# Gathers shared out between two stages, and a dense stage of a graph network rebuilt around centred matmul outputs

## The reference

```python
h = relu(layernorm(x)); x = x + L0(h, node_type, src, dst, etype, ...)  # typed attention, softmax over a node's edges
h = relu(layernorm(x)); x = x + L1(h, proj_cosim, W_ffn, b_ffn, src, dst)  # relu(h_diff @ W_ffn.T + b_ffn)
h = relu(layernorm(x)); x = x + L2(h, edge_index, W0, b0, W1, b1)
h = relu(layernorm(x)); x = x + L3(h, Wq, ..., Wf, bf, gamma, beta, src, dst)

def L2(x, edge_index, W0, b0, W1, b1):
    h = x + segment_sum(x[src], dst)
    return relu(h @ W0 + b0) @ W1 + b1

def L3(feats, ...):                       # o: attention over the edges, 0 for a node without any, + bo
    h = feats @ Wf + bf + o
    return h + (h - mean(h)) * rsqrt(var(h) + 1e-5) * gamma + beta
```

## Time and profile before

| | us |
|---|---|
| median of 3 runs | 6195.22 (6193.31 to 6201.44) |
| the profiled execution | 6195.52, span 6193.7 |
| tables | 0 to 167 |
| dense | 167 to 1397 |
| scores | 1400 to about 2407 |
| granted clock, mean | 0.788 of 2.4 GHz |

### The profile page before, as it was taken

One profiled execution on the slowest core, in us unless ns is written; L12 is line 12 of the kernel. 1 busy time (PEld: TensorE's weight loads), 2 busy tenths in 40 slices (PEclk: granted clock), 3 DMA queues, 4 the chain that ended last, 5 costly groups with the idle time before them and its releaser, 6 DMA issues. The chain is left out here.

```text
span 6193.7 us, 73617 instructions
## 1 busy us (share of the span) xinstructions
PE 5013.1 (81%) x19049; PEld 2686.4 (43%) x19049; DVE 4517.1 (73%) x7949; ACT 2488.5 (40%) x7048; POOL 3864.5 (62%) x3983
## 2 busy tenths in 40 slices
PE   0899489988999996999978886666688877878886
PEld 0455245544555553566644443222233334444443
DVE  4788377767888886999966665666688766666666
ACT  0788367763333332455533332222233333333333
POOL 1777787764444441000058887888788857777787
PEclk9999688889999998999965555555688866777666
DMA  9333145543333332999943333444566622222221
GB/s 357 109 105 105 34 134 136 136 119 80 81 80 79 81 80 46 277 286 285 285 108 83 83 83 79 115 114 114 121 164 165 156 75 66 65 65 64 63 59 41
DMA packets 868574, 739.52 MB, mean 119 GB/s; under 512 B 568092, under 2 KB 575218, under 8 KB 868032
## 3 DMA queue, kind: packets, MB, share of 16 engines
q1 hardware_dynamic: 566112, 525.53, 29.8%
q0 software_dynamic: 102464, 90.84, 8.1%
q10 hardware_dynamic: 199584, 118.45, 6.3%
HBM read 461.89 MB, written 276.55 MB: 119 GB/s over the span
## 5 line engine op out<-in xcount | busy, mean ns | idle before, releaser
L1298 POOL DMA_INDIRECT df_hs<-u,keep_idx x396 | 510.0, 1288 | 829.4 <-POOLq L209 709.1
L832 POOL DMA_INDIRECT sc_xg<-t,keep_gather x396 | 466.2, 1177 | 546.1 <-DVE sc_h L194 413.8
L748 POOL DMA_INDIRECT t<-keep_ptr_pay,keep_scat_ptr x396 | 472.1, 1192 | 253.4 <-issue 128.8
L1298 POOL DMA_INDIRECT hd_gat<-u,keep_idx x396 | 487.2, 1230 | 157.0 <-issue 115.2
L758 POOL DMA_INDIRECT den_xd<-t,keep_gather x396 | 474.3, 1198 | 122.3 <-issue 115.8
L1831 POOL DMA_INDIRECT out_x<-hd_x,keep_scat_out x396 | 451.0, 1139 | 146.7 <-issue 119.1
L1298 POOL DMA_INDIRECT pr_gat<-sd,keep_idxsd x396 | 411.8, 1040 | 88.8 <-issue 70.8
L1298 POOL DMA_INDIRECT ml_gat<-u,keep_idx x396 | 401.1, 1013 | 98.6 <-issue 70.3
L629 ACT ACTIVATE den_dh<-den_den_dn_cent,den_den_dn_rstd 128x64 f32<-128x64 f32 x1584 | 397.8, 335 | 4.8 <-DVE den_den_dn_rstd L609 0.5
L1287 PE MATMUL at_ps_m<-at_vx,keep_msg_twice 128*128 128x512 f32 x792 | 364.2, 603 | 24.4 <-DVE at_vx L1178 24.4
L981 PE MATMUL sc_ps_r<-sc_qx,keep_weights 128*64 128x512 f32 x792 | 361.1, 598 | 1.0 <-DVE sc_prod L896 1.0
(11 more groups left out here) (297 smaller groups left out, 13083.3 us busy)
## 6 DMA issues: line engine op xcount, KB each, us to landing
u<-den_dh SPq DMA_DIRECT2D x198, 256.0 KB
t<-tab_row ACTq DMA_DIRECT2D x99, 272.0 KB, 11.3
tab_x<-in_x SPq DMA_DIRECT2D x99, 256.0 KB
den_dx<-in_x SPq DMA_DIRECT2D x99, 256.0 KB
out_x<-den_dx SPq DMA_DIRECT2D x99, 256.0 KB
sc_et<-in_etype_row SPq DMA_DIRECT2D x99, 256.0 KB
at_v<-vt SPq DMA_DIRECT2D x198, 128.0 KB, 5.4
at_et<-in_etype_row SPq DMA_DIRECT2D x99, 256.0 KB
```

Of the source, the lines that this page charges most:

```text
L748: pool.indirect_dma_start(pairs, bass.IndirectOffsetOnAxis(ap=e.scat_ptr[:, c:c + 1], axis=0), e.ptr_pay[:, c, :], None, bounds_check=NP * ...
L832: pool.indirect_dma_start(xg[i][:, u, :], None, e.T0, bass.IndirectOffsetOnAxis(ap=e.gather0[:, b.n, u:u + 1], axis=0), bounds_check=NP - ...
L1298: pool.indirect_dma_start(gat[i][:, u, :], None, table, bass.IndirectOffsetOnAxis(ap=idx_all[:, c:c + 1], axis=0), bounds_check=rows - 1, ...
```

## The change

**POOL and SP.** EARLY = 56 of the 99 groups of target gathers stay in dense, the other 43 (LATE, spread evenly, never two neighbours) go to scores, where POOL gathers them straight into the slot that DVE reads, behind the group's four source gathers; SP no longer loads such a group from XD but stores it there, since a later stage reads it. In dense the scatters and gathers run without waiting for the steps, with six buffers instead of three, and SP's stores of gathered rows begin at step 66 instead of 49.

The diff, cut to its core:

```diff
@@ constants and tables
+EARLY = 56
+LATE = [b for b in range(NG) if b * (NG - EARLY) // NG != (b + 1) * (NG - EARLY) // NG]
...
+                def exact_thirds(to, half, bias):
+                    link(v.tensor_copy(left[:, :], bias))
+                    link(v.memset(total[:, :], 0.0))
+                    for third in range(3):
+                        link(v.tensor_copy(piece[:, :], left[:, :]))
+                        link(v.tensor_copy(wide[:, :], piece[:, :]))
+                        link(v.tensor_tensor(left[:, :], left[:, :], wide[:, :], ALU.subtract))
+                        link(v.scalar_tensor_tensor(out=total[:, :], in0=wide[:, :], scalar=e.C["ident"][:, third:third + 1],
+                                                    in1=total[:, :], op0=ALU.mult, op1=ALU.add))
+                    link(v.tensor_copy(to[:, :, half, :], total[:, :].unsqueeze(1).broadcast_to([P, TU, D])))
...
@@ Dense.vector
         if part == 0:
+            if self.on(f1):
+                n3.recip(v, f1)
             if self.on(d):
...
+            if self.on(f1):
+                k = RN - self.ON_V
+                v.scalar_tensor_tensor(out=self.h3[f1.s][:, k:RN, :], in0=self.c3[f1.n % 2][:, k:RN, :], scalar=0.0,
+                                       in1=n3.rstd[:, k:RN].unsqueeze(2).broadcast_to([P, RN - k, D]),
+                                       op0=ALU.max, op1=ALU.mult).then_inc(self.h3_rows, 1)
...
+                v.tensor_tensor(self.c3[f.n % 2][:, :, :], self.ps_m[:, :, 1, :], self.c2[f.s][:, :, :], ALU.add).then_inc(self.c3_done, 1)
...
-                v.tensor_tensor(self.x2b[d.s][:, :, :], self.x2[:, :, :], self.rows(e.W["b1_row"]), ALU.add).then_inc(self.x2b_done, 1)
...
-                n3.total(v, self.x3[f.s][:, :, :]).then_inc(n3.chain, 1)
...
-                n3.shift(v, self.x3[f.s][:, :, :])
@@ Dense.tensor
                 for j in range(RN):
                     a, c = j % 2, j // 2
-                    m = pe.matmul(self.ps_m[:, j, :], self.hid[:, a, c * P:(c + 1) * P], e.W["w1"],
-                                  start=(j == 0), stop=(j == RN - 1), skip_group_check=True)
+                    if j % 4 == 0:
+                        pe.matmul(self.ps_m[:, j:j + 4, :, :], e.ones3[:, :], e.bias_m[:, :, :, :], start=True, stop=False,
+                                  skip_group_check=True)
+                    m = pe.matmul(self.ps_m[:, j, :, :], self.hid[:, a, c * P:(c + 1) * P], e.w1_pair[:, :, :],
+                                  start=False, stop=(j % 4 == 3), skip_group_check=True)
...
-                busy_with(pe, e, self.ps_idle, 3)
...
-                    pe.matmul(self.ps_h[:, 4 * bank:4 * bank + 4, :, :], e.C["ones"][0:1, :], self.e.bias_h[0:1, :, :, :],
+                    pe.matmul(self.ps_h[:, 4 * bank:4 * bank + 4, :, :], e.ones3[:, :], e.bias_h[:, :, :, :],
                               start=True, stop=False, skip_group_check=True)
@@ dense, SP
+        head = count * 66 // 99
+        def stored_at(n):
+            m, of = n - head, count - head
+            return range(len(early) * m // of, len(early) * (m + 1) // of) if 0 <= m < of else range(0)
@@ scores, POOL and SP
+                    if b.n in LATE:
+                        wait(pool, type_kept, b.n - (U - 1), e.pool_passed)
+                        wait(pool, xd_out[i], 16 * (late_of(b.n) - 1), e.pool_passed)
+                        for u in range(TU):
+                            pool.indirect_dma_start(xg[i][:, TU + u, :], None, e.T0,
+                                                    bass.IndirectOffsetOnAxis(ap=e.gather0[:, b.n, TU + u:TU + u + 1], axis=0),
+                                                    bounds_check=NP - 1, oob_is_err=False).then_inc(dst_in[i], 16)
...
+                    if b.on() and b.n in LATE:
+                        wait(sp, dst_in[b.s], 16 * TU * late_of(b.n), e.sp_passed)
+                        sp.dma_start(edge_rows(e.XD, b.n * GE, TW), xg[b.s][:, TU:R, :]).then_inc(xd_out[b.s], 16)
```

More of the change, by code:

```diff
@@ L195, in relu_to, with __init__, over, square @@
                                       op0=ALU.max, op1=ALU.mult)
+class Small:
+    def __init__(self, s, name, rows=RN):
+        self.rows = rows
+        self.sum, self.ss, self.std, self.rstd = [s.sb(f"{name}_{n}", [P, rows]) for n in ("sum", "ss", "std", "rstd")]
+        self.sq = s.sb(f"{name}_sq", [P, rows, D])
+        self.squared, self.summed, self.rooted, self.inverted = [
+            s.sem(f"{name}_{n}") for n in ("squared", "summed", "rooted", "inverted")]
+    def over(self, small):
+        return small[:, :].unsqueeze(2).broadcast_to([P, self.rows, D])
+    def square(self, a, cent, st):
+        wait(a, self.summed, st.n)
+        a.activation(self.sq[:, :, :], cent, ACT.Square).then_inc(self.squared, 1)
+    def sumsq(self, v, st):
+        v.wait_ge(self.squared, st.n + 1)
+        wait(v, self.rooted, st.n)
+        v.tensor_reduce(self.ss[:, :], self.sq[:, :, :], AX, ALU.add).then_inc(self.summed, 1)
+    def root(self, a, st, eps):
+        a.wait_ge(self.summed, st.n + 1)
+        wait(a, self.inverted, st.n)
+        a.activation(self.std[:, :], self.ss[:, :], ACT.Sqrt, bias=eps, scale=1.0 / D).then_inc(self.rooted, 1)
+    def recip(self, v, st):
+        v.wait_ge(self.rooted, st.n + 1)
+        v.reciprocal(self.rstd[:, :], self.std[:, :]).then_inc(self.inverted, 1)
 class Scope:
@@ L225, in norm @@
         return Norm(self.sb, self.sem, f"{self.tag}_{name}", rows)
-def busy_with(pe, e, ps, n):
-    for _ in range(n):
-        pe.matmul(ps[:, :], e.idle[:, 0:P], e.idle[:, :], start=True, stop=True)
 def edge_rows(table, at, width=D):
@@ L568, in vector @@
                 v.wait_ge(self.x2_done, d.n + 1)
-                n2.total(v, self.x2[:, :, :]).then_inc(n2.chain, 1)
+                wait(v, self.c2_done, d.n)
+                v.tensor_reduce(n2.sum[:, :], self.x2[d.s][:, :, :], AX, ALU.add).then_inc(self.total2, 1)
             if self.on(g):
@@ L575, in vector @@
             if self.on(g):
[L576 to L577 removed]
+                n4.recip(v, g)
             if self.on(d):
[L579 to L581 removed]
+                v.wait_ge(self.total2, d.n + 1)
+                wait(v, self.h2_done, d.n - (U - 1))
+                wait(v, self.c3_done, d.n - (U - 1))
+                v.scalar_tensor_tensor(out=self.c2[d.s][:, :, :], in0=n2.over(n2.sum), scalar=-1.0 / D,
+                                       in1=self.x2[d.s][:, :, :], op0=ALU.mult, op1=ALU.add).then_inc(self.c2_done, 1)
             if self.on(g):
[L583 removed]
+                v.wait_ge(n4.inverted, g.n + 1)
                 v.tensor_tensor(self.f1[:, :, :], self.ps_h[:, :, 0, :], n4.over(n4.rstd), ALU.mult).then_inc(self.f1_done, 1)
@@ L623, in scalar, with scale_rows @@
         eps = e.C["eps"]
-        def scale_rows(n, h, b, out, done):
-            a.wait_ge(n.chain, 2 * b.n + 2)
+        def scale_rows(n, cent, h, b, out, done, rows):
+            a.wait_ge(n.inverted, b.n + 1)
             wait(a, out[b.s], 16 * b.k)
-            for j in range(RN):
-                m = a.activation(h[b.s][:, j, :], n.cent[:, j, :], ACT.Relu, scale=n.rstd[:, j:j + 1])
+            for j in range(rows):
+                m = a.activation(h[b.s][:, j, :], cent[:, j, :], ACT.Relu, scale=n.rstd[:, j:j + 1])
             m.then_inc(done, 1)
@@ L863, in _ @@
                         wait(sp, sems[i], 16 * (NG // U), e.sp_passed)
+                for i in range(U):
+                    wait(sp, xd_out[i], 16 * late_of(NG - U + i), e.sp_passed)
             @block.vector
```

184 lines of the change are left out of this document (91 added, 93 removed).

## The result

| us | before | after |
|---|---|---|
| median on the same chip | 6194.5 (6193.3 to 6201.4) | 5954.2 (5951.3 to 5958.5) |
| the profiled execution | 6195.5 | 5958.5 (span 5956.6) |
| dense, from the issue of its first load to that of its last store | 1230.9 | 982.5 |
| scores | 1029.5 | 1035.2 |
| tables | 161 | 161 |

The ratio is 0.961, 95% interval 0.9594 to 0.9627: 240 us faster, 21 us more than forecast and inside the range. The profiled executions differ by 237.0 us: dense -248.4, scores +5.7, the stages behind them +5.4 together, none of them by over 4.3. (Scores of before runs to 2430 us; the 2407 in the table ahead of the prediction is too early.)

The account below looks back on a forecast made before the run. Dense was taken as bound by its own step, then by POOL, scores by PE. Dense -230, rough edges +5, scores +2, tables +3.3 gave -220 from 6195.2, forecast 5975 us, range 5930 to 6045.

Parts of the forecast that it names:

- The bounds of before: In dense: its own step of 10.2 us in the first half, POOL in the second, a hole between.
- The step: In dense: handoffs between ACT and DVE played at 9.58 us, kept at 9.75, saving 229.9 us over 98 steps.
- six pieces: Stretches of one dense step between ACT starts: 2.11, 1.87, 1.20, 1.80, 0.70 and 1.90 us, sum 9.58.
- the ring: In dense: the chain of handoffs through ACT and DVE that bounds the new step, 9.58 us as played.
- PE: In dense: its work per step falls from 10.0 to 7.2 us, so it leaves the bound.
- The clock: PE's granted clock in dense without idle matmuls: 0.8 to 0.86, with no time taken for it.
- Rival D: In dense: without idle matmuls PE stays at 1.2 GHz, steps of 14.4 us, slower at 6431 us; 4%.
- POOL's pace: In dense: 1.51 us per scatter or gather, possibly down to 1.45, left at 1.51.
- rival A: In dense: POOL is the bound after all, the step being 9.4 us or less, 5940 us; 17%.
- Rough edges: In the last third of dense, where stores and steps meet: +5 us, from 0 to 25.
- Rival C: Scores gets longer, DVE or PE waiting for late gathers: up to 77 us lost, 6052 us; 8%.
- Rivals B and E: B: in dense the chain doesn't shorten, steps of 10.25 us, 6024 us, 17%. E: bound lies elsewhere, 6195 us, 2%.

Follow-up runs that it names:

- the kernel with the new dense alone: Changed kernel with all 99 groups of target gathers kept in dense and stores from step 50; 6061.1 us, ratio 0.9786.
- the run with sharing alone: Kernel before with only the gathers shared out, 56 groups in dense and 43 in scores, old dense step kept; 6024.3 us, ratio 0.9727.
- the pair on another chip: Kernel with three DVE moves and 50 gather groups in dense, with and without six extra matmuls a step; 6581.9 and 6571.0 us.

## Why the prediction was right, and where its sizes were off

**The bounds of before** were read rightly: easing POOL alone, by either part, gains 143 to 179 us in dense, and doing both leaves the steps last.

**The step.** Played 9.58, kept at 9.75 for all 98 steps: -230 us against -243 measured. The mechanism and its length held. Each of the six pieces is within 0.06 us of what was played, an undisturbed step takes 9.54, and moving one pass off the ring gave 45 us. I kept 0.15 us of the old step's loss to a low clock; it is 0.19, so 94 steps take 9.73 where I had 9.75. What was missing is the end: the last four steps take 27.9 us, not 39, and that is 11 of the 13 us.

**PE.** 7.2 us of work was too much, it is 6.7 at most: a bf16 bias costs 0.22 us (3.46 / 16) where I took 0.27, and m takes 1.8 where I left it at 2.1 for safety. PE has almost 3 us to spare at full clock, so the forecast didn't hang on it. That this slack would swallow the low clock as well did not come true.

**The clock.** The forecast was 0.8 to 0.86, with nothing taken for it beside the 0.15 us above; from 200 to 690 us it is 0.91, and it costs 0.19 us a step. PE is busy 77% of that stretch, and in before, where it was busy 99%, the clock was 0.91 as well. Rival D (1.2 GHz, slower) failed by its first sign. The Trainium skill (TensorE: Matmul & The Clock Gate, "What's actually happening") has it that sustained activity is what lifts the rate; the run with six matmuls agrees in direction, 0.91 to 1.00. The price of the missing 0.09 is 2% of a step here.

**POOL's pace.** I kept 1.51 us an operation; it is 1.34. The forecast had seen that fewer two-input passes might help and priced it at 1.45. The steps were last, so nothing hung on this term, but by little: at the forecast's pace POOL's limit of 1140 us would have been only 7 us ahead of the measured last x4 pass, and the margin is wider thanks to a gain that wasn't counted. In the kernel with the new dense alone it is nearly the whole gain. The last gather starts 57 us ahead of the last x4 pass, 25 more than in before, which looks like the 26 forecast; but POOL has stood 93.5 us for the stores by then, so its own limit lies well further ahead than I had it. Two numbers of the forecast don't come out of its own rows: at 1.45 us POOL's 620 operations would be done 37 us earlier, not 10, and the 1140 us of POOL's limit ask for steps of (1140 - 211) / 98 = 9.5 us, 0.1 under the played 9.58, not 0.3, so rival A was nearer than it looked.

**The rest of the miss.** Against the profiled execution the forecast was -220 and -237.0 was measured. Rough edges (+5) and tables (+3.3) don't show. The first x4 pass comes 5.5 us earlier (205.2 against 210.7), which I hadn't counted; that the shorter steps shorten the filling of the pipeline too is my reading of it, not tested. With the step's 13 us that makes 27; scores, 3.7 above its +2, and the untouched stages, +5.4, take 9 back. Rival C's 77 us are far off: PE's cover held, and DVE waited 2.5 us for late gathers beyond its wait at the start.

**Rivals B and E** fell with the step and the result. B's case is what the run with sharing alone has: POOL eased and the old step, 10.26 us and 6024.3 us, against B's 10.25 and 6024.

**The other signs.** The last gather starts at 1090 us (1108 forecast), the last x4 pass at 1147 (1170), ACT's longest wait before the root of n4 is 1.4 us (1.3), and POOL is busy 648 us in scores (670). Scores is 5.7 us longer, just outside the 5.

## What to carry to other kernels

Where two engines hand a chain to and fro, look for work that stands behind a wait without needing it: one pass moved ahead of a reciprocal gave 45 us, three gave 80, as much as all the arithmetic that was removed gave on top of the sharing (70). Two gains that ease the same bound don't add up; count what each does alone and what is late next. Matmuls that only keep PE busy are worth a run either way: sixteen of them put PE on the bound and cost 50 us, six in the holes of after took 16 us off dense (one run, and a like difference in the pair on another chip). What the idle matmuls of before were worth by themselves wasn't tested. And a mean over all steps hides what single steps show: the step at full clock, the steps that the clock made longer, and the short ones at the end.
